# A conv-attention and expert layer for 16 images: single choice steps, half-width gate products, and w1 in reused memory

## The chip, the cores and the metric

The kernel runs on one core of one Trainium2 chip. The metric is the device time of one execution in microseconds, as the median of several runs. Everything in the kernel is float32 (or float32r, the same bits in TensorE's faster format), apart from a few bfloat16 masks.

## What is computed

The input is `x` of 16 images of 32 x 32 positions and 64 channels, so 1024 tokens of 64 channels an image. In short:

```python
# 1. convolution-style attention block
h = group_norm(x, gn_scale, gn_bias, num_groups=16)
q, k, v = nin(h, wq, bq), nin(h, wk, bk), nin(h, wv, bv)
x = x + nin(softmax(q k^T / 8) v, wo, bo)
# 2. causal attention on the layer norm
t = x.reshape(16, 1024, 64)
t = t + causal_attention(layer_norm(t), Wq, Wk, Wv)
# 3. experts choose tokens: 32 experts, 8 tokens each
u = layer_norm(t)
logits = einsum('bsd,ed->bse', u, gate_w) + gate_b
probs = softmax(logits, axis=1)            # over the 1024 tokens
topv, topi = the 8 greatest probs of each expert, and their tokens
pooled = sum over the 8 of topv * u[topi]  # (16, 32, 64)
h = gelu([pooled, 1] @ weight1[e])         # 64+1 -> 256
out = [h, 1] @ weight2[e]                  # 256+1 -> 64
t[topi] += topv * out
```

## The kernel before

The program has two parts, each a block of its own with one instruction stream an engine, ordered by semaphores; all engines meet where one block ends and the next begins. `attention_part` does steps 1 and 2, the logits, and the choice for the first three groups of images. `expert_part` does the choice of the last group, the experts, and the sum into the output.

**Turns.** `attention_part` is a pipeline over images. In turn `i` each engine walks a list written out by hand, `ORDER`, whose entries are a name and a shift: `s2.0@-1` is the piece `s2.0` for image `i - 1`. Turns run from -2 to 18. Turns 4 to 13 are a loop of five trips of two turns, in which addresses and counts are computed in registers; the others are written out. The names that matter here:

- `m1.c`, `m2.c`: TensorE products whose rows VectorE reduces to maxima (`m1r.c`, `m2r.c`, L1025), for attention 1 and 2, in the PSUM tile `maxima_in`.
- `r1`, `r2` (L589): the maxima are turned into rows in the bank `fin_ps`; `r1c`, `r2c` (L822) are ScalarE's copies to `max_rows`; `row1`, `row2` (L508) are SyncE's transfers of them into one row of `queries_lo` or `queries`. The first score of the attention, `s1.0` or `s2.0`, waits for that transfer.
- `s1.u`, `s2.u` (L677 to L681): the scores; `e1.u`, `e2.u` (L862): their exponentials on ScalarE, into `probs`; `v1.t`, `v2.t` (L696): the products with the values; `c1`, `c2` (L834) copy them.
- `ad.t` (L934): GpSimd's additions of the probabilities of attention 1; `rs1` (L597) is the product that sums them over the partitions, which waits for the last of them.
- `out1`, `out2` (L614), `f1`, `f2` (L1046), then the layer norms `l1`, `l2` on VectorE (L1054, L1059), `l1p`, `l2p` on GpSimd (L908 to L913), `l1n`, `l2n` on ScalarE (L793).
- `p2.tr` (L549), then `nh`, `nc` (L763, L766) and `nl2`, `nl1`: the normed tokens turned over into `keys`; `ya`, `yb`: the projections.
- `mtr` (L549), `ut` (L837), `mlg` (L622), `lg` (L843): the second normed tokens turned over, copied to `ut`, multiplied by the gate, and evicted with the bias to `logits`. SyncE's `sl` (L524) stores them to `logits_dram`, `su` (L518) and `st` (L513) store the normed and the plain tokens.

`ut` holds two tokens of one pair of token tiles on its 128 partitions, 64 channels each, in 512 columns. `gate_bd` is block diagonal, so that one product gives the logits of both tokens on 2 x 32 output partitions.

SyncE works its list in order too: `su@-2 st@-2 sl@-2 row2@-1 xload@+2 row1@+1`.

**The choice of experts.** Images are chosen in groups of four, so that 4 x 32 = 128 partitions hold one expert of one image each and 1024 tokens lie along a row of `lg`. The steps of a group are: `e.top` on VectorE (max of 8, its negative, match and replace, compare: L249 to L254), `e.exp` on ScalarE (L269), `e.gate` on VectorE (L257, L259), and on TensorE with a copy by ScalarE after each: `e.ta`, `e.tb` (transposes of the gates, L303), `e.pool` (64 products with `u_all`, L295), `e.turn` (L299). In turns 15 and 16 there is no image for the pieces `m1.c`, and so the choice steps of groups 0 to 2 take their places: in turn 15, two steps a piece (groups 0 and 1); in turn 16, one step a piece (group 2). A place counts from 0 to 7 in the order in which an engine's list has its `m1` pieces. Group 3 is chosen at the start of `expert_part`.

**`expert_part`.** SyncE loads the logits of group 3 (L1146), `w1` (L1148), `w2` in two halves (L1150), the bias, and the tokens `total`. TensorE waits for `w1` and for the last `e.turn`, then does the 64 hidden products (L1177), the transposes (L1188), the second products (L1198), the turn to images (L1204), and 64 products that spread the result over the tokens (L1215). VectorE adds them to `total` (L1264), and SyncE stores the output (L1163).

## Time and profile before

| | |
|---|---|
| median of 3 runs | 900.59 us (899.41 to 900.70) |
| profiled execution, its own time | 901.2 us |
| its span in the profile | 899.4 us |
| TensorE busy, share of the span | 803.9 us, 89% |
| VectorE | 566.2 us, 63% |
| ScalarE | 506.4 us, 56% |
| GpSimd | 371.0 us, 41% |
| mean TensorE clock granted | 0.941 of full speed |

The profile is of one execution. Its span runs from the first to the last instruction that the profiler shows; the time of an execution also has what lies around that. Busy time of TensorE is of pipelined instructions, whose ends are modelled. L with a number is a line of the kernel. PE is TensorE, PEld its weight loads, DVE VectorE, ACT ScalarE, POOL GpSimd, and SPq the queue of SyncE, from which the transfers are issued. What stands in brackets at the end of a row of the timeline is the time for which the engine had been idle and what released it.

### The profile page before, as it was taken

What the parts mean: (1) busy time and instruction counts of PE and PEld (TensorE: products, weight loads), DVE (VectorE), ACT (ScalarE), POOL (GpSimd) and SP (SyncE); (2) the same over time, 40 slices, a digit from 0 to 9 for tenths busy, and PEclk for the clock granted to TensorE, in tenths of its full rate; (3) what the DMA queues carried; (4) which work ended last, traced back from release to release, by engine and by line L of the source; (5) the groups of instructions that cost most, each with busy time, mean ns of one, the idle gap of its engine ahead of it and who ended that gap; (6) DMA issues with size and microseconds to landing.
All of it is one profiled execution on the core that took longest, in us unless ns stands there. A gap on an engine that the chain in (4) does not pass through costs nothing. (4 is left out here: it accounts for less than half of the span.)

```text
span 899.4 us, 14859 instructions
## 1 busy us (share of the span) xinstructions
PE 803.9 (89%) x4406; PEld 473.2 (53%) x4406; DVE 566.2 (63%) x1493; ACT 506.4 (56%) x1096; POOL 371.0 (41%) x288
## 2 busy tenths in 40 slices
PE   4586999999999999999999999999999997755286
PEld 2253556565656565656565656565656553433155
DVE  3427476767676767676767676767777755451224
ACT  3153567676767666666676666666666663533120
POOL 3062536363636364545454545455454543100000
PEclk9997899999999999999999999999999998958558
DMA  1000000000000000000000000000000020010798
GB/s 46 0 1 12 1 13 25 18 24 19 24 19 24 19 24 18 24 18 24 18 24 18 24 18 24 18 24 18 24 18 24 7 71 30 1 31 1 147 239 230
DMA packets 62997, 30.54 MB, mean 34 GB/s; under 512 B 35279, under 2 KB 60271, under 8 KB 62959
## 3 DMA queue, kind: packets, MB, share of 16 engines
q1 hardware_dynamic: 62959, 30.05, 13.5%
q8 instruction: 21, 0.34, 0.2%
q14 instruction: 17, 0.14, 0.1%
HBM read 15.23 MB, written 10.49 MB: 29 GB/s over the span
## 5 line engine op out<-in xcount | busy, mean ns | idle before, releaser
L1025 DVE TENSOR_REDUCE neg_max<-maxima_in 128x1 f32<-128x1024 f32 (+7 forms) x256 | 252.0, 984 | 94.3 <-PE maxima_in L654 90.8
L862 ACT ACTIVATE probs<-scores 128x512 f32<-128x512 f32 (+3 forms) x464 | 233.0, 541 | 118.0 <-PE scores L681 106.4
L934 POOL TENSOR_TENSOR prob_sum<-prob_sum,probs 128x1024 f32<-128x1024 f32 x96 | 228.2, 2377 | 8.8 <-ACT probs L862 0.6
L654 PE MATMUL maxima_in<-keys,queries 128*128 128x512 f32 (+3 forms) x496 | 172.6, 422 | 17.3 <-DVE neg_max L1025 14.4
L681 PE MATMUL scores<-queries,keys 128*128 128x512 f32 (+3 forms) x464 | 173.0, 373 | 0.0
L654 PEld LDWEIGHTS maxima_in<-keys,queries 128*128 128x128 f32 x496 | 85.9, 200 | 89.9 <-DVE neg_max L1025 57.4
L696 PE MATMUL values_out<-probs,x_sb 128*64 128x512 f32 x512 | 129.4, 612 | 0.0
L908 POOL TENSOR_TENSOR ln<-ln_mv,eps_ln 128x8 f32<-128x8 f32 x32 | 6.5, 203 | 297.8 <-DVE ln_mv L1059 297.8
L679 PE MATMUL scores<-queries_lo,keys_hi 65*128 65x512 f32 x256 | 109.8, 429 | 2.2 <-DMA queries_lo<-max_rows 1.2
L681 PEld LDWEIGHTS scores<-queries,keys 128*128 128x128 f32 x464 | 90.5, 195 | 8.2
L696 PE MATMUL values_out<-probs,normed 128*64 128x128 f32 (+3 forms) x480 | 84.5, 441 | 0.1
L679 PE MATMUL scores<-queries_lo,keys 128*128 128x512 f32 (+3 forms) x208 | 80.4, 388 | 0.0
L793 ACT ACTIVATE u_sb<-t,ln 128x64 f32<-128x64 f32 x128 | 44.2, 427 | 30.0 <-POOL ln L913 30.0
L679 PEld LDWEIGHTS scores<-queries_lo,keys_hi 65*128 65x128 f32 x256 | 49.8, 195 | 17.1 <-ACT probs L862 6.8
L934 POOL TENSOR_TENSOR prob_sum<-probs 128x1024 f32<-128x1024 f32 x16 | 37.8, 2361 | 50.4 <-ACT probs L862 50.4
L919 POOL TENSOR_TENSOR x_bias<-x_sb,bias_full 128x512 f32<-128x512 f32 x16 | 20.9, 1304 | 89.8 <-DVE t L1046 87.0
L696 PEld LDWEIGHTS values_out<-probs,x_sb 128*64 128x64 f32 x512 | 28.8, 136 | 53.4 <-issue 41.3
L911 POOL TENSOR_TENSOR ln<-ln,minus_half 128x8 f32<-128x8 f32 x32 | 52.6, 1642 | 0.0
L696 PEld LDWEIGHTS values_out<-probs,normed 128*64 128x64 f32 x480 | 30.2, 137 | 36.9 <-issue 26.9
L793 ACT ACTIVATE normed<-t,ln 128x63 f32<-128x63 f32 x128 | 44.0, 427 | 7.7 <-POOL ln L913 7.1
L679 PEld LDWEIGHTS scores<-queries_lo,keys 128*128 128x128 f32 x208 | 41.4, 199 | 2.4 <-ACT probs L862 0.2
L1012 DVE SCALAR_TENSOR_TENSOR keys<-proj_ps,bias_qk,keys 64x512 fp32r<-64x512 f32 x32 | 24.2, 757 | 25.5 <-ACT keys L806 25.5
(169 smaller groups left out, 1102.7 us busy)
## 6 DMA issues: line engine op xcount, KB each, us to landing
x_sb<-in_x SPq DMA_DIRECT2D x16, 256.0 KB, 2.9
u_all<-u_sb SPq DMA_DIRECT2D x16, 256.0 KB, 2.5
t_scratch<-t SPq DMA_DIRECT2D x16, 256.0 KB, 2.9
total<-t_scratch SPq DMA_DIRECT2D x16, 256.0 KB, 4.8
w_sb<-in_w SPq DMA_DIRECT2D x1, 2080.0 KB
logits_scratch<-logits SPq DMA_DIRECT2D x32, 64.0 KB, 2.1
lg<-logits_scratch SPq DMA_DIRECT2D x4, 512.0 KB, 3.7
out<-total SPq DMA_DIRECT2D x16, 128.0 KB, 2.2
```

What stands on the lines that cost most here:

```text
L654: mm = pe.matmul(maxima_in[:, lo:lo + w * P], weights, keys[s][q][:, h * HALF:h * HALF + w * P], start=not diagonal, stop=True, skip_group ...
L679: pe.matmul(shape(bank), low_keys[:, key_cols(t)], of(queries_lo[s][q]), start=not diagonal, stop=False, skip_group_check=diagonal)
L681: pe.matmul(shape(bank), keys[s][q][:, key_cols(t)], of(queries[s][q]), start=False, stop=True, skip_group_check=diagonal).then_inc(scores ...
L696: mm = pe.matmul(values_out[a * C:(a + 1) * C, j0 * P:HALF], v_sb[:, t, :], probs[:, t % NP, a * HALF + j0 * P:(a + 1) * HALF], start=t == ...
L793: ins = nc.scalar.activation(dst[:, t, 0:width], src[:, t, 0:width], ACT.Identity, bias=ln[s][:, 0, t:t + 1], scale=ln[s][:, 1, t:t + 1])
L862: nc.scalar.activation(of(probs[:, t % NP, :]), shape(scores[:, bank_of(s, u), 0:w]), ACT.Exp, scale=SCALE).then_inc(exp_done, 1)
L908: nc.gpsimd.tensor_tensor(ln[s][:, 0, :], ln_mv[s][:, :, 1], eps_ln[:, :], ALU.add).then_inc(norm_step[s], 1)
L911: nc.gpsimd.tensor_tensor(ln[s][:, 1, :], ln[s][:, 0, :], minus_half[:, :], ALU.pow).then_inc(norm_step[s], 1)
L919: nc.gpsimd.tensor_tensor(x_bias[:, :, :], x_sb[n.parity][:, :, :], bias_full[n.parity][:, :].unsqueeze(1).to_broadcast([P, NT, C]), ALU.a ...
L934: nc.gpsimd.tensor_tensor(prob_sum[:, :], before, probs[:, t % NP, :], ALU.add).then_inc(rows_added, 1)
L1012: V.scalar_tensor_tensor(out=keys[1][q][C:P, c], in0=proj_ps[C:P, :], scalar=bias_qk[C:P, 1:2], in1=keys[1][q][C:P, c], op0=ALU.add, op1=A ...
L1025: V.tensor_reduce(neg_max[s][:, at:at + 1], maxima_in[:, HALF - widths[0] * P:HALF + widths[1] * P], AX.X, ALU.max, negate=True).then_inc( ...
```

## The change

- **Choice in single steps over two turns.** `e.top` is split into `e.max`, `e.rep` and `e.ne`. A table, `EXPERT_SLOTS`, says for each engine which steps stand in which of 16 places (0 to 7 in turn 15, 8 to 15 in turn 16). Each group has its own semaphore `expert_step[k]`, and waits between groups stand where tiles are shared (`rest`, `gates_t`, the PSUM halves).
- **ScalarE's order.** `lg@-2` now stands ahead of place 0, `r2c@-1` behind place 1, and `l1n` ahead of places 5 and 6.
- **Gate product in halves.** `mlg` is two products of 256 columns, on output partitions 0 to 63 and 64 to 127; `logits` is 128 x 256, evicted in one piece; `sl` stores it in four transfers. `gate_b_sb` has 128 partitions, loaded by four transfers.
- **The last logits straight into their tile.** For image 15, `mlg` writes to partitions 96 to 127 of two banks, and `lg` puts them with two evictions into `lg`. `sl` is left out for it, and SyncE loads the other three images of group 3 right after `su` of image 15.
- **w1 into memory that is no longer read.** The tiles of attention 1 (`keys`, `queries`, `keys_hi`, `queries_lo`) lie in one region, and `w1_sb` lies over them. ScalarE issues its load after `e1.15` of image 15, in turn 15.

The diff, without what only renames semaphores:

```diff
--- before.py
+++ after.py
@@ -35,9 +36,9 @@
     "act": "e1.0 e1.1 e1.2 e1.3 e1.4 xh@+1 e1.5 e1.6 l2n@-2 e1.7 xc@+1 e1.8 e1.9 ab@+1 wh@+1 e1.10 ws@+1 e1.11 "
-        "ka.hi@+1 e1.12 e1.13 kb.hi@+1 e1.14 ut@-2 qa.hi@+1 e1.15 m1.0@+1 lg@-2 r2c@-1 m1.1@+1 c1 m1.2@+1 e2.0@-1 "
-        "e2.1@-1 m1.3@+1 e2.2@-1 qb.hi@+1 e2.3@-1 e2.4@-1 m1.4@+1 e2.5@-1 e2.6@-1 kB@+1 e2.7@-1 e2.8@-1 m1.6@+1 "
-        "l1n m1.5@+1 e2.9@-1 e2.10@-1 nh e2.11@-1 nc m1.7@+1 e2.12@-1 ya.hi c2@-1 r1c@+1 yb.hi",
+        "ka.hi@+1 e1.12 e1.13 kb.hi@+1 e1.14 ut@-2 qa.hi@+1 e1.15 lg@-2 m1.0@+1 m1.1@+1 r2c@-1 c1 m1.2@+1 e2.0@-1 "
+        "e2.1@-1 m1.3@+1 e2.2@-1 qb.hi@+1 e2.3@-1 e2.4@-1 m1.4@+1 e2.5@-1 e2.6@-1 kB@+1 e2.7@-1 e2.8@-1 l1n "
+        "m1.5@+1 m1.6@+1 e2.9@-1 e2.10@-1 nh e2.11@-1 nc m1.7@+1 e2.12@-1 ya.hi c2@-1 r1c@+1 yb.hi",
...
@@ -95,10 +96,21 @@
 NG = B // BG
-EXPERT_STEPS = ["e.top", "e.exp", "e.gate", "e.ta", "e.tb", "e.pool", "e.turn"]
-EXPERT_STEP_COUNT = {"e.top": ["max", "neg", "rest", "chosen"], "e.exp": [], "e.gate": ["recip", "gates"],
+EXPERT_STEPS = ["e.max", "e.exp", "e.rep", "e.ne", "e.gate", "e.ta", "e.tb", "e.pool", "e.turn"]
+EXPERT_STEP_COUNT = {"e.max": ["max", "neg"], "e.exp": [], "e.rep": ["rest"], "e.ne": ["chosen"], "e.gate": ["recip", "gates"],
...
+EXPERT_SLOTS = {
+    "dve": {0: [("e.max", 0)], 1: [("e.rep", 0)], 2: [("e.ne", 0)], 3: [("e.gate", 0)], 4: [("e.max", 1)], 5: [("e.rep", 1)],
+            6: [("e.ne", 1)], 7: [("e.gate", 1)], 8: [("e.max", 2)], 9: [("e.rep", 2)], 10: [("e.ne", 2)], 11: [("e.gate", 2)]},
+    "act": {2: [("e.exp", 0)], 5: [("e.ta", 0)], 6: [("e.exp", 1), ("e.tb", 0)], 7: [("e.pool", 0)], 8: [("e.turn", 0)],
+            9: [("e.ta", 1)], 10: [("e.exp", 2), ("e.tb", 1)], 11: [("e.pool", 1)], 12: [("e.turn", 1), ("e.ta", 2)],
+            13: [("e.tb", 2)], 14: [("e.pool", 2)], 15: [("e.turn", 2)]},
+    "pe": {5: [("e.ta", 0)], 6: [("e.tb", 0)], 7: [("e.pool", 0)], 8: [("e.turn", 0)], 9: [("e.ta", 1)], 10: [("e.tb", 1)],
+           11: [("e.pool", 1)], 12: [("e.turn", 1), ("e.ta", 2)], 13: [("e.tb", 2)], 14: [("e.pool", 2)], 15: [("e.turn", 2)]},
+}
...
@@ -106,11 +118,7 @@
     c = [piece for piece, _ in pieces].index(name)
-    if n == B:
-        return [(EXPERT_STEPS[k % 7], k // 7) for k in (2 * c, 2 * c + 1) if k < 14]
-    if n == B + 1 and c < 7:
-        return [(EXPERT_STEPS[c], 2)]
-    return []
+    return EXPERT_SLOTS[engine].get(c + NT * (n - B), [])
...
@@ -225,8 +233,12 @@
         pooled = sb("pooled", [C + 1, E, 32])
+        base = -(-nc.sbuf_base // 64) * 64
+        region = sb("region", [P, 8 * S + 16])
+        w1_sb = nc.alloc_sbuf_tensor_at("w1_sb", [C + 1, E, HID], F32, offset=base)
+        w1_loaded = whole.enter_context(nc.semaphore("w1_loaded"))
         logits_loaded = [whole.enter_context(nc.semaphore(f"logits_loaded{k}")) for k in range(NG)]
-        expert_step = whole.enter_context(nc.semaphore("expert_step"))
+        expert_step = [whole.enter_context(nc.semaphore(f"expert_step{k}")) for k in range(NG)]
...
@@ -236,20 +248,26 @@
-    V, step, lg, rest, top, stat, gates = (nc.vector, *(g[n] for n in ("expert_step", "lg", "rest", "top", "stat", "gates")))
+    V, lg, rest, top, stat, gates = (nc.vector, *(g[n] for n in ("lg", "rest", "top", "stat", "gates")))
+    step = g["expert_step"][k]
...
     def after(step_name):
-        before = done("expert_step", name, k, step_name, back=1)
+        before = done(f"expert_step{k}", name, k, step_name, back=1)
...
-    if name == "e.top":
-        after("max")
+    if name == "e.max":
...
         V.tensor_scalar(stat[:, k, 0:1], top[:, k, 0:1], -1.0, None, ALU.mult).then_inc(step, 1)
+    elif name == "e.rep":
+        if k > 0:
...
+            V.wait_ge(g["expert_step"][k - 1], done(f"expert_step{k - 1}", "e.gate", k - 1, "gates"))
+        after("rest")
         V.match_replace(rest[:, :], top[:, k, :], lg[:, k % 2, :], NEG_HUGE).then_inc(step, 1)
+    elif name == "e.ne":
...
@@ -283,12 +302,16 @@
-    pe, step, gates, gates_t, u_all, pool_sb, ident_f = (nc.tensor, *(
-        g[n] for n in ("expert_step", "gates", "gates_t", "u_all", "pool_sb", "ident_f")))
+    pe, gates, gates_t, u_all, pool_sb, ident_f = (nc.tensor, *(
+        g[n] for n in ("gates", "gates_t", "u_all", "pool_sb", "ident_f")))
+    step = g["expert_step"][k]
...
-    pe.wait_ge(step, done("expert_step", name, k, EXPERT_STEP_COUNT[name][0]) - 1)
+    if name == "e.ta" and k > 0:
...
+        pe.wait_ge(g["expert_step"][k - 1], done(f"expert_step{k - 1}", "e.turn", k - 1, "copy"))
+    pe.wait_ge(step, done(f"expert_step{k}", name, k, EXPERT_STEP_COUNT[name][0]) - 1)
...
@@ -325,10 +348,11 @@
-    keys = {s: [sb(f"keys{s}{q}", [P, S], F32R) for q in range(2)] for s in (1, 2)}
-    queries = {s: [sb(f"queries{s}{q}", [P, S], F32R) for q in range(2)] for s in (1, 2)}
-    keys_hi = [sb(f"keys_hi{q}", [C + 1, S], F32R) for q in range(2)]
-    queries_lo = {1: [sb(f"queries_lo1{q}", [C + 1, S], F32R) for q in range(2)],
+    in_region = lambda name, k, rows: nc.alloc_sbuf_tensor_at(name, [rows, S], F32R, offset=g["base"] + 4 * S * k)
+    keys = {1: [in_region(f"keys1{q}", q, P) for q in range(2)], 2: [sb(f"keys2{q}", [P, S], F32R) for q in range(2)]}
+    queries = {1: [in_region(f"queries1{q}", 2 + q, P) for q in range(2)], 2: [sb(f"queries2{q}", [P, S], F32R) for q in range(2)]}
+    keys_hi = [in_region(f"keys_hi{q}", 4 + q, C + 1) for q in range(2)]
+    queries_lo = {1: [in_region(f"queries_lo1{q}", 6 + q, C + 1) for q in range(2)],
...
@@ -354,7 +378,7 @@
     ut = sb("ut", [P, HALF])
-    logits = sb("logits", [2 * E, HALF])
+    logits = sb("logits", [P, HALF // 2])
...
@@ -395,7 +419,7 @@
                    (channel_consts[second, :], g["by_channel"]), (rows[:, 0, :], g["bo"]),
-                   (gate_b_sb[0:E, :], g["gate_b"]), (gate_b_sb[E:2 * E, :], g["gate_b"])]
+                   *[(gate_b_sb[r * E:(r + 1) * E, :], g["gate_b"]) for r in range(P // E)]]
...
@@ -483,15 +507,15 @@
-        def load_logits(k):
...
-            sp.wait_ge(logits_stored, 32 * (k + 1) * BG)
+        def load_logits(k, images=BG):
...
+            sp.wait_ge(logits_stored, 64 * (k * BG + images))
...
-                sp.wait_ge(g["expert_step"], done("expert_step", "e.top", k - 2, "chosen"))
+                sp.wait_ge(g["expert_step"][k - 2], done(f"expert_step{k - 2}", "e.ne", k - 2, "chosen"))
                 sp.wait_ge(g["exp_ready"], k - 1)
-            sp.dma_start(g["lg"][:, k % 2, :], logits_dram[k * BG:(k + 1) * BG].rearrange("b e s -> (b e) s")).then_inc(
-                g["logits_loaded"][k], 16)
+            sp.dma_start(g["lg"][0:images * E, k % 2, :],
+                         logits_dram[k * BG:k * BG + images].rearrange("b e s -> (b e) s")).then_inc(g["logits_loaded"][k], 16)
...
@@ -516,13 +540,15 @@
                 sp.dma_start(u_dst, u_sb[:, :, :].rearrange("p t c -> p (t c)")).then_inc(u_stored, 16)
-            elif name == "sl":
+                if n.trip is None and n.first == B - 1:
+                    load_logits(NG - 1, BG - 1)
+            elif name == "sl" and (n.trip is not None or n.first < B - 1):
...
                 sp.wait_ge(fin_step, ready)
-                dst = image_of(logits_dram, at).rearrange("e (j a t) -> a e j t", a=2, t=P)
-                for a in range(2):
-                    sp.dma_start(dst[a], logits[a * E:(a + 1) * E, :].rearrange("e (j t) -> e j t", t=P)).then_inc(
-                        logits_stored, 16)
+                dst = image_of(logits_dram, at).rearrange("e (h j a t) -> h a e j t", h=2, a=2, t=P)
+                for h, a in itertools.product(range(2), range(2)):
+                    r = (2 * h + a) * E
+                    sp.dma_start(dst[h, a], logits[r:r + E, :].rearrange("e (j t) -> e j t", t=P)).then_inc(logits_stored, 16)
...
@@ -617,9 +643,19 @@
                 transposes(fin_ps, u_sb).then_inc(fin_step, 1)
+            elif name == "mlg" and n.trip is None and n.first == B - 1:
...
+                pe.wait_ge(proj_step, done("proj_step", "yb", n, "lo"))
+                for a, bank in enumerate((fin_ps, proj_ps)):
+                    r = slice(a * C, (a + 1) * C)
+                    mm = pe.matmul(bank[P - E:P, :], gate_bd[r, a * E:(a + 1) * E], ut[r, :], start=True, stop=True)
+                mm.then_inc(fin_step, 1)
...
-                pe.matmul(fin_ps[0:2 * E, :], gate_bd[:, :], ut[:, :], start=True, stop=True).then_inc(fin_step, 1)
+                for h in range(2):
+                    mm = pe.matmul(fin_ps[h * 2 * E:(h + 1) * 2 * E, 0:HALF // 2], gate_bd[:, :],
+                                   ut[:, h * HALF // 2:(h + 1) * HALF // 2], start=True, stop=True)
+                mm.then_inc(fin_step, 1)
...
@@ -835,12 +871,20 @@
                 nc.scalar.copy(ut[:, :], fin_ps[:, :]).then_inc(fin_step, 1)
+            elif name == "lg" and n.trip is None and n.first == B - 1:
+                act.wait_ge(fin_step, done("fin_step", "mlg", n, "mm"))
+                act.wait_ge(g["expert_step"][NG - 3], done(f"expert_step{NG - 3}", "e.ne", NG - 3, "chosen"))
+                for a, bank in enumerate((fin_ps, proj_ps)):
+                    ins = nc.scalar.activation(
+                        g["lg"][P - E:P, (NG - 1) % 2, :].rearrange("p (j a t) -> p a j t", a=2, t=P)[:, a, :, :],
+                        bank[P - E:P, :].rearrange("p (j t) -> p j t", t=P), ACT.Identity, bias=gate_b_sb[P - E:P, :], scale=1.0)
+                ins.then_inc(fin_step, 1)
...
-                    act.wait_ge(logits_stored, each(n + (-1), 32))
-                nc.scalar.activation(logits[:, :], fin_ps[0:2 * E, :], ACT.Identity, bias=gate_b_sb[:, :],
+                    act.wait_ge(logits_stored, each(n + (-1), 64))
+                nc.scalar.activation(logits[:, :], fin_ps[:, 0:HALF // 2], ACT.Identity, bias=gate_b_sb[:, :],
...
@@ -861,6 +905,9 @@
                                  scale=SCALE).then_inc(exp_done, 1)
+            if s == 1 and u == len(UNITS[1]) - 1 and n.trip is None and n.first == B - 1:
...
+                nc.scalar.dma_start(g["w1_sb"][:, :, :], g["w1"].rearrange("e d h -> d e h")).then_inc(g["w1_loaded"], 16)
...
@@ -1142,10 +1189,6 @@
     def _(sp):
-        k = LAST_GROUP
-        sp.dma_start(g["lg"][:, k % 2, :], logits_dram[k * BG:(k + 1) * BG].rearrange("b e s -> (b e) s")).then_inc(
-            g["logits_loaded"][k], 16)
-        sp.dma_start(w1_sb[:, :, :], g["w1"].rearrange("e d h -> d e h")).then_inc(w1_loaded, 16)
```

## Rows read from the trace of the kernel before

**Rows 1.** Windows: busy time of each engine, weight loads second; clock; DMA.

```profile
400.00:700.00 300.00, 299.00 (x1592) 176.59 (x1593) 216.08 (x587) 202.12 (x443) 149.97 (x112) 1.00 0.08 20
...
740.00:760.00 20.00, 13.49 (x104) 6.43 (x107) 10.86 (x12) 7.13 (x13) 10.29 (x5) 0.83 0.11 33
```

**Rows 2.** The chain that ended last: start, length, what.

```profile
840.84 16.03 DMA w_sb<-in_w
...
856.91 7.05 PE hidden_ps L1177 x64
```

**Rows 3.** Timeline, start of the kernel: start, length, engine, instruction.

```profile
3.65 0.78 SPq L475 DMA_DIRECT2D gate_b_sb<-in_gate_b  x2
...
6.05 1.11 PE L549 MATMUL proj_ps<-masks_f,x_sb 128*128 128x128 f32 x4 [6.05 <-DMA gate_b_sb<-in_gate_b]
```

**Rows 4.** Timeline of TensorE in a loop turn, and one earlier row.

```profile
611.68 1.07 PE L622 MATMUL fin_ps<-ut,gate_bd 128*64 128x512 f32 x2
612.68 0.73 PE L654 MATMUL maxima_in<-keys,queries 128*128 128x512 f32 x2
...
617.55 0.23 PE L677 MATMUL scores<-mask_k,ident_b 128*128 128x128 bf16 x1
...
720.74 1.08 PE L696 MATMUL values_out<-probs,normed 128*64 128x256 f32 x8
```

**Rows 5.** Timeline of ScalarE in that loop turn.

```profile
611.91 0.59 ACT L862 ACTIVATE probs<-scores 128x512 f32<-128x512 f32 x1
612.87 0.68 ACT L843 ACTIVATE logits<-fin_ps,gate_b_sb 64x512 f32<-64x512 f32 x1 [0.37 <-PE fin_ps L622]
```

**Rows 6.** Timeline of SyncE in that loop turn.

```profile
613.72 1.48 SPq L524 DMA_DIRECT2D logits_scratch<-logits  x2
615.32 0.73 SPq L508 DMA_DIRECT2D queries<-max_rows  x1
```

**Rows 7.** Timeline: the first transfer of maxima and the score behind it.

```profile
45.14 0.78 SPq L508 DMA_DIRECT2D queries_lo<-max_rows  x1
47.08 0.28 PEld L679 LDWEIGHTS scores<-queries_lo,keys_hi 65*128 65x128 f32 x1 [1.61 <-DMA queries_lo<-max_rows]
```

**Rows 8.** Timeline of turn 3, which is written out.

```profile
205.55 1.28 SPq L524 DMA_DIRECT2D logits_scratch<-logits  x2
...
209.60 0.23 PE L677 MATMUL scores<-mask_k,ident_b 128*128 128x128 bf16 x1
```

**Rows 9.** Timelines of GpSimd, ScalarE and TensorE in turn 15.

```profile
735.97 14.89 POOL L934 TENSOR_TENSOR prob_sum<-prob_sum,probs 128x1024 f32<-128x1024 f32 x6
...
747.65 1.15 ACT L269 ACTIVATE gates<-lg,stat 128x1024 f32<-128x1024 f32 x1 [1.53 <-DVE stat L251]
...
748.80 0.67 ACT L843 ACTIVATE logits<-fin_ps,gate_b_sb 64x512 f32<-64x512 f32 x1
...
749.52 0.39 PE L589 MATMUL fin_ps<-masks_f,neg_max 128*8 128x128 f32 x2 [2.17 <-ACT logits L843]
...
760.33 0.23 PE L677 MATMUL scores<-mask_k,ident_b 128*128 128x128 bf16 x1
...
773.60 2.75 ACT L793 ACTIVATE normed<-t,ln 128x63 f32<-128x63 f32 x8
```

**Rows 10.** Timeline of SyncE at the start of the second part.

```profile
840.84 0.40 SPq L1148 DMA_DIRECT2D w_sb<-in_w  x1
841.53 16.72 SPq L1150 DMA_DIRECT2D w_sb<-in_w  x2
```

**Rows 11.** Timeline of TensorE: one group's pooling, turn 16.

```profile
814.48 1.10 PE L295 MATMUL maxima_in<-u_all,gates_t 128*32 128x64 f32 x64
```

**Rows 12.** Timeline around the change of block.

```profile
836.50 0.68 ACT L843 ACTIVATE logits<-fin_ps,gate_b_sb 64x512 f32<-64x512 f32 x1 [2.06 <-PE fin_ps L622]
...
844.18 1.23 DVE L249 MAX8 top<-lg 128x8 f32<-128x1024 f32 x1 [16.77 <-DMA lg<-logits_scratch]
...
855.80 0.26 ACT L277 COPY pooled<-small_ps 64x128 f32<-64x128 f32 x1 [0.51 <-PE small_ps L299]
```

More of the change, by code:

```diff
@@ L1 @@
+import itertools
 from contextlib import ExitStack
@@ L169, in count_increments @@
             for step in EXPERT_STEP_COUNT[name]:
-                inc("expert_step", (name, k, step))
+                inc(f"expert_step{k}", (name, k, step))
     return counts
@@ L217, in build_program @@
         ident_f = masks_f[:, 1, :]
-        gate_b_sb = sb("gate_b_sb", [2 * E, 1])
+        gate_b_sb = sb("gate_b_sb", [P, 1])
         lg = sb("lg", [P, 2, S])
@@ L263, in choose_on_scalar @@
 def choose_on_scalar(nc, g, name, k, turn, pool_ps):
-    step, gates, gates_t, pool_sb, pooled = (g[n] for n in ("expert_step", "gates", "gates_t", "pool_sb", "pooled"))
+    gates, gates_t, pool_sb, pooled = (g[n] for n in ("gates", "gates_t", "pool_sb", "pooled"))
+    step = g["expert_step"][k]
     if name == "e.exp":
-        nc.scalar.wait_ge(step, done("expert_step", "e.top", k, "neg"))
+        nc.scalar.wait_ge(step, done(f"expert_step{k}", "e.max", k, "neg"))
         nc.scalar.activation(gates[:, k, :], g["lg"][:, k % 2, :], ACT.Exp, bias=g["stat"][:, k, 0:1], scale=1.0,
@@ L271, in choose_on_scalar @@
     elif name in ("e.ta", "e.tb", "e.pool", "e.turn"):
-        nc.scalar.wait_ge(step, done("expert_step", name, k, EXPERT_STEP_COUNT[name][0]))
+        nc.scalar.wait_ge(step, done(f"expert_step{k}", name, k, EXPERT_STEP_COUNT[name][0]))
         if name == "e.pool":
@@ L536, in _ @@
         sp.wait_ge(u_stored, 16 * B)
-        sp.wait_ge(logits_stored, 32 * B)
+        sp.wait_ge(logits_stored, 64 * (B - 1))
     @block.tensor
@@ L635, in piece @@
                 name, k = in_bank.pop("step")
-                pe.wait_ge(g["expert_step"], done("expert_step", name, k, "copy"))
+                pe.wait_ge(g["expert_step"][k], done(f"expert_step{k}", name, k, "copy"))
             block_c = c if s == 1 else query_block(c)
@@ L1117, in sem @@
         return ctx.enter_context(nc.semaphore(name))
-    w1_sb = sb("w1_sb", [C + 1, E, HID])
+    w1_sb, w1_loaded = g["w1_sb"], g["w1_loaded"]
     w2_sb = sb("w2_sb", [P, E, 2, C])
@@ L1172, in _ @@
         pe.wait_ge(w1_loaded, 16)
-        pe.wait_ge(expert_step, done("expert_step", "e.turn", LAST_GROUP, "copy"))
+        pe.wait_ge(expert_step[LAST_GROUP], done(f"expert_step{LAST_GROUP}", "e.turn", LAST_GROUP, "copy"))
         for quad in range(QUADS):
```

5 lines of the change are left out of this document (3 added, 2 removed).

## The prediction

> **What bounds the kernel now.** I read the windows first. Between 400 and 700 us TensorE is busy 299.00 of 300 us at full clock [rows 1]: in the middle of the kernel, whatever takes TensorE longer, or makes it wait, is paid in full. Between 740 and 760 us it is busy only 13.49 of 20 us and its clock falls to 0.83: there the drained pipeline is bound by hand-overs. Then the chain that ended last [rows 2]: in its last 60 us it goes back to one transfer, w1, 16.03 us long, before the hidden product L1177. So four places count: the start, the loop turns, turns 15 and 16, and the tail. I read each in the timeline.
>
> **Start.** `gate_b_sb` now needs four loads instead of two. The two take SyncE 0.78 us to issue, and the first TensorE instruction waits for them at 6.05 us [rows 3]. Two more: **+0.8 us**. Nothing hides it. The bounds are 0.6 and 1.0.
>
> **The logits in each turn: product, eviction, stores.** Before, the product L622 holds TensorE from 611.68 to 612.68 us, two passes of 512 columns on 64 output columns [rows 4]. Now it is two products of 256 columns, each on its own half of the output partitions. The nearest row is eight such passes in 1.08 us [rows 4], so four take about 0.5: TensorE gains 0.5 us a turn, if nothing else holds it. It gains nothing if the halves run one after the other.
>
> The eviction L843 starts at 612.87 and takes 0.68 us [rows 5]. With an earlier product it can start when the exponential before it ends, 611.91 + 0.59 = 612.50, and 256 fewer elements a partition save some 0.2 us: it ends near 613.01, not 613.55, 0.54 us sooner. Bounds: 0.2 and 0.6.
>
> The stores grow from two to four on SyncE, and `row2`, the transfer of the maxima of attention 2, stands behind them in SyncE's order. In a loop turn two issues take 1.48 us [rows 6]; two more add 1.49. `row2` was issued at 615.32 and now goes at 615.32 - 0.54 + 1.49 = 616.27. What such a transfer takes is seen once, where TensorE waits for it: issued at 45.14, work begins at 47.08 [rows 7], 1.94 us, and I take 1.9. So before, `row2` landed near 617.22 and `s2.0` began at 617.55 [rows 4] without a wait, 0.33 us to spare. Now it lands near 618.17, while TensorE, 0.5 us earlier, would be there at 617.05. The wait swallows the half microsecond and makes the turn 0.62 us longer. Behind `s2.0` in TensorE's order stand all scores, values and out1, and behind those VectorE's f1 and l1, so it isn't made up. The loop has 10 turns: **+6.2 us**. The other three turns (2, 3, 14) are written out and have no register work between the issues: two take 1.28 us, and `s2.0` follows at 209.60 [rows 8]. Four end near 205.55 - 0.54 + 2.62 = 207.63, the row lands near 209.5, in time: 0. Bounds of the whole term: with issues of 0.39 us as in [rows 3] the row is hidden and 13 turns give up to -5; with no gain from the product and eviction it is +12. I stay with 0.74 an issue, since it is the same tile and destination.
>
> The Trainium skill (DMA: Bandwidth & Descriptors, section on the anatomy of one DMA, written for GpSimd's path) puts the sequencer's dispatch at about 50 ns and calls descriptor generation small; by that, two more stores would cost SyncE 0.1 us and the row would stay hidden, which is the second case below. The rows of this case show 0.6 to 0.7 us an issue, ten times that.
>
> **Turn 15 (no image 16; experts of groups 0 and 1).** Before, ScalarE does the first choice's exponential at 747.65, waiting for VectorE's max, before the eviction of the logits at 748.80; the product `r2` at 749.52 waits for that eviction, and `s2.0` of image 14 begins at 760.33, behind a gate product, transposes and the pooling [rows 9]. Now the eviction stands ahead of the choice, and TensorE's first expert step comes at slot 5, after `v2.1`. What is late next is GpSimd: its last row addition ends at 735.97 + 14.89 = 750.86 [rows 9], the row sums wait for it, and `row2` behind four stores lands near 751.6. So `s2.0` begins near 752.0: -8.3. Between there and the layer norm L793 at 773.60 [rows 9] the second group's max, replace, compare and exponential leave the path too: VectorE's single steps fall in the gaps between f1, l1 and nl2, ScalarE's copies come behind that norm. I get it near 762; but then copy, exponential of group 1 and a second copy (0.6 + 1.3 + 0.6) stand ahead of the next projections' eviction, so that from there on the lead is **-10.2 us**. If w1's traffic delays `row2` by 3 us it is -7; if nothing of the copies counts, -12.
>
> **w1.** Its load is now issued by ScalarE after `e1.15` of image 15. On SyncE the issue took 0.40 us [rows 10]; behind it ScalarE's queue has the logits' eviction, for which `r2` waits, with 4 us to spare against GpSimd's end. I cost it at nothing. The memory it lands in was the first attention's keys and queries, dead by then.
>
> **Turn 16.** Moved here: pooling and turning of group 1, with group 2's steps later. Of it, TensorE's pooling is 1.10 us [rows 11] (up to 1.9 at the lower clock), the turn 0.3, and group 2's transposes now wait for ScalarE's copy of that turn, some 0.5 beyond what the score banks cost anyhow: about 2 us. Two extra copies on ScalarE before `row2`'s source cost 0.3. **+2.3 us**, bounds 0.5 and 4.5. VectorE's steps there lie in its idle time beside the scores.
>
> **Tail.** Before: the logits' eviction ends at 836.50 + 0.68 = 837.18, and the max of group 3 starts at 844.18, after store, block change and load [rows 12]: 7.0 us. Now three images are loaded during the layer norm's tail, and image 15 goes from the two banks into the tile. That adds a second product (its rows and bank differ; 0 to 2 us, I take 0.5), a second eviction 0.6 and a block change 0.3: 1.4 us, so -5.6. From max to the last copy, 855.80 + 0.26 = 856.06 [rows 12], nothing changes; then w1 was waited for until 856.91 [rows 2], which goes: -0.85. **-6.4 us**, bounds -4 and -7. What is late next is w2, but it is needed only behind the 7.05 us of L1177 and the transposes, and now isn't queued behind w1. The sums and output stores keep their pace.
>
> **Sum.** 0.8 + 6.2 - 10.2 + 2.3 - 6.4 = -7.3 us. The profiled execution took 901.2 us (span 899.4 and 1.8 around it), 0.6 above the median of 900.59. 901.2 - 7.3 = 893.9, as a median **893.3 us**.
>
> **The rivals.**
>
> 1. The row is late in the loop: 893.3, own range 888 to 898. For it: 1.49 us of issue against 0.33 of slack. Chance 0.50.
> 2. The row stays hidden, since an issue with half the blocks is shorter or the transfer lands sooner. Then the loop gives -5 instead of +6.2: 893.3 - 11.2 = 882. With partial hiding 887. For it: [rows 3] has issues of 0.39. Chance 0.27.
> 3. w1's transfer, 16 us on the same DMA engines, holds up `row2` of image 14 (and the late row costs more than I think): +3, some 896 to 898. The Trainium skill (DMA: Bandwidth & Descriptors, "Issuing engines are not separate DMA queues") says that transfers issued by different engines interleave on the same 16 engines. No row of before has such a small transfer beside a large one of another queue. Chance 0.10.
> 4. The final choice doesn't start sooner, because the block's end still waits for stores: only w1's 0.85 of the tail is gained, 899. Against it: only the stores of the tokens remain, which are issued ahead of the logits. Chance 0.06.
> 5. Slower: ScalarE is held while it issues w1. The two w2 loads held SyncE for 16.72 us [rows 10]. In turn 15 ScalarE has some 4 us of cover; each further one goes onto the end, so above 4 + 7.3, about 11 us, the kernel is slower; at 16.7 it is 906. Against it: w1's own 0.40. Chance 0.07.
>
> **Chances and range.** Faster by over 0.2%: cases 1 to 4, less a little for mishaps, 0.91. Within 0.2%, which is about what a measurement of this kernel can tell from no change: 0.02. Slower: 0.07. The range reaches down to case 2 and up to cases 3 and 4: 882 to 900.
>
> **What would show it.** The first TensorE instruction at 6.8 us. In loop turns four issues of L524's successor over 2.9 us, and `s2.0` waiting some 1.1 us for the DMA of `max_rows`; each such turn 0.62 us longer. The logits' product at 0.5 us. In turn 15, `s2.0` of image 14 near 1.2 us behind GpSimd's last addition, and not ten. The max of group 3 1.4 us after the last eviction, L1177 with no DMA wait. The prediction is wrong if the wait at `s2.0` isn't there (then near 882), if ScalarE's w1 issue is longer than a few us, or if the block change waits.

## The result, and the profile after

The changed kernel takes **884.28 us** as the median of 4 runs (882.52 to 888.38), the kernel before 900.64 beside it (899.41 to 902.65). The ratio is 0.9824, with a 95% interval of 0.9800 to 0.9849. The forecast was 893.3 us, with a range of 882 to 900. The sign was right and the time lies in the range, but the gain is 16.4 us, more than twice the 7.3 that the sum gave. A second set of runs of the same kernel gave 888.46 (884.72 to 891.23) against 900.26, ratio 0.9864 (0.9825 to 0.9902). Over the eight runs of both sets the mean is 886.5.

The profiled execution took 884.59 us, with a span of 882.8. In the middle of the kernel the windows view looks as in [rows 1] (busy time of TensorE, its weight loads, VectorE, ScalarE and GpSimd, then clock, DMA share and GB/s): TensorE is the bound, at full clock. From 740 to 760 us the clock and TensorE's busy time are a little lower than in [rows 1], and the DMA share has gone from 0.11 to 0.65. That is w1's transfer, which now lies in this stretch.

```profile
400.00:700.00 300.00, 299.01 (x1614) 177.63 (x1616) 217.89 (x589) 202.72 (x446) 152.40 (x113) 1.00 0.08 20
...
740.00:760.00 20.00, 12.75 (x63) 7.12 (x62) 9.78 (x21) 6.77 (x14) 7.70 (x4) 0.74 0.65 140
```

**A loop turn.** First TensorE's timeline, then SyncE's, of the changed kernel, in the turn of [rows 4] and [rows 6].

```profile
609.97 0.65 PE L656 MATMUL fin_ps<-ut,gate_bd 128*64 128x256 f32 x4
610.56 0.73 PE L690 MATMUL maxima_in<-keys,queries 128*128 128x512 f32 x2
...
615.42 0.23 PE L713 MATMUL scores<-mask_k,ident_b 128*128 128x128 bf16 x1
```

```profile
611.39 1.84 SPq L551 DMA_DIRECT2D logits_scratch<-logits  x4
613.34 0.69 SPq L532 DMA_DIRECT2D queries<-max_rows  x1
```

The product takes 0.59 us of TensorE from its start to the next, not 1.00 as in [rows 4]. Four stores take 1.84 us, 0.46 each, where two took 1.48. (A block is 128 tokens of one expert that lie together; a store had 32 x 4 = 128 of them and has 64 now.) `row2` is issued 1.95 us after the first store instead of 1.60, and `s2.0` at 615.42 has no idle time in brackets: it didn't wait. Counted from the start of the gate product, the first store is 0.62 us sooner than before (1.42 instead of 2.04), so `row2` is 0.27 us sooner (3.37 instead of 3.64) and `s2.0` 0.42 (5.45 instead of 5.87).

**Turn 15.** TensorE's timeline, ScalarE's queue, SyncE's, and what the DMA view of 742 to 762 us says.

```profile
748.28 1.08 PE L623 MATMUL fin_ps<-prob_sum,ones_f 128*32 128x256 f32 x8 [2.77 <-POOL prob_sum L981]
753.83 0.29 PE L713 MATMUL scores<-mask_k,ident_b 128*128 128x128 bf16 x1 [4.47 <-DMA queries<-max_rows]
```

```profile
742.78 0.63 ACTq L910 DMA_DIRECT2D w_sb<-in_w  x1
```

```profile
745.90 0.65 SPq L532 DMA_DIRECT2D queries<-max_rows  x1
```

```profile
q10 hardware_dynamic: 2093, 2.13, 52.1%
q1 hardware_dynamic: 480, 0.66, 12.9%
```

Here is a wait that the forecast sum doesn't have. `s2.0` of image 14 stands 4.47 us for a row of 4 KB, issued at 745.90 and usable at 753.83: 7.9 us instead of the 1.9 of [rows 7]. In the second trace it stands 5.29 us. In that stretch w1's queue, q10, takes 52% of the DMA engines' time.

**The change of part and the tail.** VectorE's and ScalarE's timelines, then the chain that ended last.

```profile
831.03 0.66 ACT L878 ACTIVATE lg<-proj_ps,gate_b_sb 32x512 f32<-32x512 f32 x1
```

```profile
832.04 1.23 DVE L261 MAX8 top<-lg 128x8 f32<-128x1024 f32 x1 [10.66 <-PEq L243]
```

```profile
844.21 4.84 PE hidden_ps L1220 x64
...
852.91 4.15 PE small_ps L1241 x128
...
860.08 15.82 PE hidden_ps L1258 x64
```

The max of group 3 follows the end of the last eviction by 0.35 us; it was 7.0 in [rows 12]. Nothing of w1 stands in the chain any more, and the hidden product takes 4.84 us, not the 7.05 of [rows 2]; this difference is also seen without an edit (after_again, below).

**The span cut up.** The gate's product (`mlg`) of image 0, 13, 14 and 15 and the hidden product cut each trace into six stretches. Each row is one profiled execution, in us; the numbers are differences of start times in TensorE's timeline. The kernels are those of the experiments below.

| kernel | to image 0 | 0 to 13 | 13 to 14 | 14 to 15 | 15 to hidden product | to the end | span |
|---|---|---|---|---|---|---|---|
| before | 158.49 | 586.93 | 52.84 | 36.23 | 22.42 | 42.5 | 899.4 |
| after | 160.68 | 581.99 | 48.15 | 37.66 | 15.73 | 38.6 | 882.8 |
| after, again | 158.64 | 581.77 | 48.34 | 37.26 | 16.03 | 43.9 | 885.9 |
| halves_only | 160.62 | 581.68 | 51.57 | 35.62 | 21.82 | 44.2 | 895.5 |
| no_halves | 158.57 | 586.96 | 49.15 | 38.25 | 15.99 | 44.4 | 893.3 |
| no_w1 | 159.50 | 581.87 | 43.18 | 36.66 | 18.86 | 43.8 | 883.9 |
| w1_later | 159.98 | 581.61 | 41.99 | 37.37 | 15.88 | 44.1 | 880.9 |
| no_steps | 160.73 | 581.98 | 51.45 | 35.46 | 15.96 | 40.7 | 886.3 |
| no_last | 160.67 | 582.03 | 48.55 | 37.44 | 20.85 | 42.2 | 891.7 |
| eight_stores | 158.57 | 615.53 | 48.13 | 38.19 | 15.97 | 41.2 | 917.6 |
| eight_row_first | 160.40 | 581.46 | 46.04 | 37.29 | 15.88 | 44.0 | 885.1 |
| best1 | 159.80 | 581.65 | 41.58 | 37.68 | 15.86 | 38.7 | 875.3 |
| best1, again | 158.13 | 581.85 | 40.65 | 37.63 | 16.21 | 44.2 | 878.7 |
| best2 | 158.99 | 581.59 | 42.01 | 37.31 | 16.05 | 43.9 | 879.9 |

The first and the last stretch differ by up to 2.6 and 5.8 us whatever the edit, and between executions of one kernel as well. The four in between repeat within 0.4 us in the two executions of the changed kernel and within 0.9 in those of best1, and in them the parts of the change can be read one by one.

### The profile page after: what moved, and what is told of

Same layout as the page of the kernel before. It is cut to its first block and busy times, and to the rows that moved or that the text cites. A ratio compares the mean times of both kernels' runs of the same rounds, so it can differ in the third digit from the quotient of the medians.

```text
span 882.8 us, 14997 instructions
## 1 busy us (share of the span) xinstructions
PE 796.8 (90%) x4438; PEld 474.7 (54%) x4438; DVE 564.6 (64%) x1493; ACT 503.7 (57%) x1097; POOL 370.2 (42%) x288
## 5 line engine op out<-in xcount | busy, mean ns | idle before, releaser
L717 PE MATMUL scores<-queries,keys 128*128 128x512 f32 (+3 forms) x464 | 175.1, 377 | 0.0
L732 PE MATMUL values_out<-probs,x_sb 128*64 128x512 f32 x512 | 127.5, 608 | 0.0
L829 ACT ACTIVATE u_sb<-t,ln 128x64 f32<-128x64 f32 x128 | 44.2, 428 | 29.9 <-POOL ln L960 29.9
L732 PEld LDWEIGHTS values_out<-probs,x_sb 128*64 128x64 f32 x512 | 28.5, 135 | 53.3 <-issue 38.7
L829 ACT ACTIVATE normed<-t,ln 128x63 f32<-128x63 f32 x128 | 44.1, 426 | 9.0 <-POOL ln L960 9.0
```

The lines of the kernel that those rows point to most:

```text
L717: pe.matmul(shape(bank), keys[s][q][:, key_cols(t)], of(queries[s][q]), start=False, stop=True, skip_group_check=diagonal).then_inc(scores ...
L732: mm = pe.matmul(values_out[a * C:(a + 1) * C, j0 * P:HALF], v_sb[:, t, :], probs[:, t % NP, a * HALF + j0 * P:(a + 1) * HALF], start=t == ...
L829: ins = nc.scalar.activation(dst[:, t, 0:width], src[:, t, 0:width], ACT.Identity, bias=ln[s][:, 0, t:t + 1], scale=ln[s][:, 1, t:t + 1])
```

## The experiments

**halves_only**: only the product, eviction and four stores of the change; choice steps, last logits and w1 as before.

```diff
-            if s == 1 and u == len(UNITS[1]) - 1 and n.trip is None and n.first == B - 1:
-                nc.scalar.dma_start(g["w1_sb"][:, :, :], g["w1"].rearrange("e d h -> d e h")).then_inc(g["w1_loaded"], 16)
+        sp.dma_start(w1_sb[:, :, :], g["w1"].rearrange("e d h -> d e h")).then_inc(w1_loaded, 16)
...
+EXPERT_SLOTS = {engine: OLD_SLOTS for engine in ("dve", "act", "pe")}
...
-            elif name == "mlg" and n.trip is None and n.first == B - 1:
...
-            elif name == "lg" and n.trip is None and n.first == B - 1:
```

The first pair is no_w1 below, the second no_steps, the third no_last.

> The changed kernel with three of its parts undone: choice steps as before, last logits by way of memory, w1 loaded in the second part. Left of the change: gate product in halves, four stores of logits, four loads of the bias, and attention 1's tiles in one region. Theory A (a store with half the blocks is issued in some 0.46 us, so the row of maxima stays hidden and TensorE keeps its half microsecond a turn): 900.6 + 0.5 at the start - 13 x 0.43 = 895.5, with s2.0 of the loop turns without a wait. Theory B (the prediction's: the row is late in the loop): 907. Theory C (the loop's gain comes from something else than the halves, the tiles' place in memory): 895.5 too, and the next kernel tells it from A.

Measured: 897.1 us (ratio 0.9959, 0.9943 to 0.9975). The stretch from image 0 to 13 is 581.68 us, 5.25 shorter than before, with no wait for the row in a loop turn. The halves give 0.4 us a turn; the late row of the forecast isn't there. (907 would have been the time with it.)

**no_halves**: the change without them.

```diff
-                for h in range(2):
-                    mm = pe.matmul(fin_ps[h * 2 * E:(h + 1) * 2 * E, 0:HALF // 2], gate_bd[:, :],
-                                   ut[:, h * HALF // 2:(h + 1) * HALF // 2], start=True, stop=True)
+                pe.matmul(fin_ps[0:2 * E, :], gate_bd[:, :], ut[:, :], start=True, stop=True).then_inc(fin_step, 1)
```

> The changed kernel with the gate product whole again and two stores of logits of 64 x 512; all else stays. Theory A: the loop turns are 45.35 us again, not 44.93; 884.3 + 5 = 889. Theory C (tiles' place in memory): the turns stay at 44.93 and the time at 884 to 885.

Measured: 894.8 us (0.9923, 0.9897 to 0.9949). 586.96 us from image 0 to 13, the number of before to 0.03. (The 889 us of the forecast are 6 short.) So the loop's gain comes from the halves alone, and not from the tiles' new place in memory or anything else that moved. The whole time is 8.3 us above the changed kernel's mean of 886.5. The two profiled executions differ by more, 10.5 us, twice what the loop accounts for; the table puts 5.8 of it into the last stretch, where the clock differed (below).

**no_w1**: w1 loaded at the start of the second part again. **w1_later**: ScalarE issues it after the first exponential of attention 2 of image 14, which is behind the row that it held up.

```diff
-            if s == 1 and u == len(UNITS[1]) - 1 and n.trip is None and n.first == B - 1:
+            if s == 2 and u == 0 and n.trip is None and n.first == B - 2:
                 nc.scalar.dma_start(g["w1_sb"][:, :, :], g["w1"].rearrange("e d h -> d e h")).then_inc(g["w1_loaded"], 16)
```

> The changed kernel with w1 loaded by SyncE at the start of the second part, ahead of w2, into the same memory. Theory D (w1's traffic holds up the row of maxima of image 14 in turn 15, which landed 7.9 us after its issue): that transfer lands in 2 us, s2.0 of image 14 waits no more than 0.3 us for it, which gives back 4.4 us; and the hidden product waits for w1 until some 16.5 us after the second part's start, 4 us longer than now, and runs at the lower clock again, 2.2 us more. Sum 884.3 - 4.4 + 4 + 2.2 = 886. Rival E (the row was late for another reason, four stores ahead of it): s2.0 still waits 4 us, 890.

> The changed kernel with ScalarE's issue of w1 moved behind the first exponential of attention 2 of image 14, so behind the row of maxima of that turn. Theory D: s2.0 of image 14 starts at once behind the row sums, 4.4 us earlier, and nothing small is in flight while w1 lands: 884.3 - 4.4 = 880. Rival E: no change, 884. A third way: the transfer now collides with the loads of logits of group 2, which isn't needed for 40 us, so no cost.

Measured: 884.98 us (0.9824, 0.9803 to 0.9845) and 879.34 us (0.9762, 0.9745 to 0.9779). TensorE's timeline of w1_later in turn 15:

```profile
747.21 1.08 PE L623 MATMUL fin_ps<-prob_sum,ones_f 128*32 128x256 f32 x8 [2.78 <-POOL prob_sum L981]
748.22 0.29 PE L713 MATMUL scores<-mask_k,ident_b 128*128 128x128 bf16 x1
```

`s2.0` follows the row sums without a gap. From image 13 to 14 it is 43.18 us without w1 and 41.99 with w1 later, against 48.15 and 48.34 in the two traces of the changed kernel: w1's transfer costs 5.0 to 6.4 us there. In no_w1 some 3 us come back in the tail (18.86 us from the last gate product to the hidden one, against 15.73 and 16.03), where the chain that ended last holds the transfer again:

```profile
824.87 15.15 DMA w_sb<-in_w
840.07 7.05 PE hidden_ps L1218 x64
```

So w1 at the chosen place gains nothing that the times show over not moving it; issued seven microseconds later, at 749.60, it gives a median 5 us lower.

**no_steps**: the old cutting of the choice into seven steps a turn apart, and ScalarE's old order. The table of slots becomes:

```diff
+OLD_STEPS = [["e.max", "e.rep", "e.ne"], ["e.exp"], ["e.gate"], ["e.ta"], ["e.tb"], ["e.pool"], ["e.turn"]]
+OLD_SLOTS = {c: [(name, k // 7) for k in (2 * c, 2 * c + 1) if k < 14 for name in OLD_STEPS[k % 7]] for c in range(8)}
+OLD_SLOTS.update({8 + c: [(name, 2) for name in OLD_STEPS[c]] for c in range(7)})
```

> The changed kernel with the old cutting of the choice (seven steps a turn apart, the gate's value and the exponentials after it on the old turns) and ScalarE's old order. Theory E (the choice as single operations takes GpSimd's product out of the way of the last images' softmax sums): the stretch between the gate products of images 13 and 14, 52.8 us before and 48.2 after, goes back to about 52.5, and w1's transfer hides in it; the loop keeps its period of 44.9. 884.3 + 4.5 = 889. Rival: the row behind w1's transfer sets that stretch whichever way the choice is cut: 884 to 885.

Measured: 887.83 us (0.9857, 0.9819 to 0.9896). 13 to 14 takes 51.45 us, 3.3 more than with the new steps, and 14 to 15 takes 35.46, 2.2 less. In the interval of the times it can't be told from the changed kernel. The theory had 52.5 us for the first of these stretches and 889 for the whole. With w1 in the way, the new steps are worth about 1 us. Without it they are worth much more: halves_only has the old steps and 51.57 + 35.62 = 87.2 us, no_w1 the new ones and 79.8. With the old steps w1's early load costs nothing (51.45 us with it, 51.57 in halves_only without): `s2.0` comes so late there that the row is in place.

**no_last**: the last image's logits stored and loaded back like the others.

```diff
-            elif name == "mlg" and n.trip is None and n.first == B - 1:
...
-            elif name == "lg" and n.trip is None and n.first == B - 1:
...
-                if n.trip is None and n.first == B - 1:
-                    load_logits(NG - 1, BG - 1)
...
+        sp.dma_start(g["lg"][:, k % 2, :], logits_dram[k * BG:(k + 1) * BG].rearrange("b e s -> (b e) s")).then_inc(
+            g["logits_loaded"][k], 16)
```

> The changed kernel with the last image's logits stored and loaded back as the others, the load at the head of the second part. Theory F (the gap at the change of parts is the round trip of the last logits): the last choice starts 7.0 us after the last eviction and not 0.35, so +6.65 and some 0.7 for the plain store: 891. Rival (the load of w1 and w2 would be awaited at the second part's start anyway): 884 to 886; against it stands that w1 is already there and w2 is wanted only 8 us later.

Measured: 891.17 us (0.9883, 0.9845 to 0.9920). VectorE's timeline:

```profile
837.26 1.23 DVE L261 MAX8 top<-lg 128x8 f32<-128x1024 f32 x1 [15.66 <-DMA lg<-logits_scratch]
```

The eviction ended at 829.86 + 0.47 = 830.33, so the gap is 6.9 us again; from the last product to the hidden one it is 20.85 us instead of 15.73 to 16.03. Doing without the round trip through memory is worth 5 us.

**eight_stores** and **eight_row_first**: each turn's logits in eight stores of 32 blocks, with SyncE's order as it is and with `row2` ahead of the stores.

```diff
-                for h, a in itertools.product(range(2), range(2)):
+                for h, a, j in itertools.product(range(2), range(2), range(2)):
                     r = (2 * h + a) * E
-                    sp.dma_start(dst[h, a], logits[r:r + E, :].rearrange("e (j t) -> e j t", t=P)).then_inc(logits_stored, 16)
+                    sp.dma_start(dst[h, a, :, j, :], logits[r:r + E, j * P:(j + 1) * P]).then_inc(logits_stored, 16)
```

```diff
-    "sp": "su@-2 st@-2 sl@-2 row2@-1 xload@+2 row1@+1",
+    "sp": "su@-2 st@-2 row2@-1 sl@-2 xload@+2 row1@+1",
```

> The changed kernel with each turn's logits stored in eight transfers of 32 blocks instead of four of 64. Two and four stores took 0.74 and 0.46 us of SyncE each. Theory G (an issue has a fixed part of about 0.18 us and 0.0044 us a block, from 128 blocks in 0.74 and 64 in 0.46): 8 x 0.32 = 2.6 us, row2 issued 0.7 us later than now, at the edge of hidden, so the loop moves by 0 to +0.3 us a turn: 884 to 889. Rival (an issue costs the same 0.46 us whatever it holds): 3.7 us a turn, row2 1.8 us later, TensorE waits 1.0 to 1.8 us at s2.0 in each turn: 884 + 13 x 1.4 = 902.

> Eight stores of 32 blocks again (922 us with the stores ahead of row2), and SyncE's order swapped so that row2's issue goes ahead of the stores. Theory G2 (all of the 37 us that eight stores added is the row that arrives 2 us late in each turn; the stores themselves hold up nobody): the turn goes back to 44.9 us and the time to 884 to 887. Rival (the small transfers themselves, 64 blocks more per turn on the queue and on SyncE, slow the loop): over 900.

Measured: 922.03 us (1.0240, 1.0205 to 1.0274) and 885.78 us (0.9819, 0.9789 to 0.9850). The theory's slope over blocks was wrong, and the rival's price was nearly right (0.50 us a store for 0.46); but the rival's time, 902, was 20 us short. SyncE's and TensorE's timelines of eight_stores:

```profile
636.38 3.99 SPq L551 DMA_DIRECT2D logits_scratch<-logits  x8
640.48 0.68 SPq L532 DMA_DIRECT2D queries<-max_rows  x1
```

```profile
642.54 0.22 PE L713 MATMUL scores<-mask_k,ident_b 128*128 128x128 bf16 x1 [1.97 <-DMA queries<-max_rows]
```

Here is the late row that the forecast expected, with its mark in brackets, 2.06 us behind its issue. It makes the 13 turns 615.53 - 581.99 = 33.5 us longer, 2.6 us a turn, more than the 1.8 that TensorE waits per turn at this place from 400 to 700 us. The windows from image 0 to 13, of the changed kernel and of eight_stores, and three microseconds behind one of the waits, say where the rest is:

```profile
160.68:742.67 581.99, 579.68 (x3115) 341.11 (x3114) 419.49 (x1144) 388.00 (x850) 293.38 (x220) 1.00 0.09 22
158.57:774.10 615.53, 591.78 (x3115) 351.03 (x3114) 420.06 (x1144) 388.76 (x850) 293.33 (x220) 0.98 0.09 21
...
690.00:693.00 3.00, 3.00 (x13) 2.81 (x13) 1.27 (x7) 1.11 (x2) 0.00 (x0) 0.50 0.18 41
```

TensorE has the same 3115 products on record, but is idle 23.8 us instead of 2.3 and busy 591.8 instead of 579.7. So 21.4 of the 33.5 us are the waits, and 12.1 are the same work at a lower clock: behind seven of the loop's ten waits the granted clock falls to 0.50 for some microseconds. With the row ahead of the same eight stores the 13 turns are back at 581.46, so the small transfers themselves cost nobody anything. Between 13 and 14 eight_row_first still stands behind w1:

```profile
752.52 0.29 PE L713 MATMUL scores<-mask_k,ident_b 128*128 128x128 bf16 x1 [3.97 <-DMA queries<-max_rows]
```

**best1**: w1_later, with the four `gate_b` loads behind the second image and a semaphore of their own, for which only `lg` waits. **best2**: best1 with `row2` ahead of the stores.

```diff
-                   *[(gate_b_sb[r * E:(r + 1) * E, :], g["gate_b"]) for r in range(P // E)]]
+                   ]
...
         sp.dma_start(x_sb[1][:, :, :], xv[1]).then_inc(x_loaded[1], 16)
+        for r in range(P // E):
+            sp.dma_start(gate_b_sb[r * E:(r + 1) * E, :], g["gate_b"]).then_inc(gate_b_loaded, 16)
...
             elif name == "lg":
+                act.wait_ge(gate_b_loaded, 64)
```

> w1 issued by ScalarE after the first softmax piece of image 14 (as in w1_later, 879.3) and the four loads of gate_b behind the second image, on a semaphore of their own that only the first eviction of logits waits for. The four loads took 1.71 us of SyncE ahead of TensorE's start at 6.59. Theory H (the first wait ends with the last of these loads, and the whole kernel follows it): TensorE starts at 4.9 to 5.2 and all else 1.4 us sooner: 878. Rival (the start is bound by the 256 KB image that lands at about 5.9 whatever stands behind it): 879.

> best1 (w1 behind the first softmax piece of image 14, gate_b off the start) with row2's issue ahead of the four stores. max_rows is ready at 612.99 in the turn where the row is now issued at 613.34, and the first scores start at 615.42, 0.03 us after the row lands. Theory (the row is just hidden with four stores): nothing to gain in the loop, at most 0.1 us a turn, 877 to 879. Rival (the row is what the turn waits for, and TensorE's order merely hides it): 0.3 us a turn sooner, 873 to 875.

Measured: 878.73 us (0.9761, 0.9722 to 0.9800) and 881.48 (0.9776, 0.9750 to 0.9802). TensorE starts at 5.82 us in best1 (6.26 when it ran again) instead of 6.59, its wait now ended by the load of `bo`; SyncE's 1.7 us don't come back in full, and in the time nothing shows: w1_later has the same ratio. The intervals of w1_later and best1 lie below those of the changed kernel, or just touch them: over its two sets best1 has a mean of 878.3 us in eight runs, where the changed kernel has 886.5. best2 gains nothing over it: its median is some 3 us higher (best1 had 877.82 in the same set), which neither of its forecasts had and which stays unexplained. Its 581.59 us from image 0 to 13 say that with four stores the row is hidden.

**best1_again** and **after_again**: the same two kernels once more.

> The kernel of best1 once more (878.7 us). Theory K (the granted clock of the second part differs from one execution to the next of the same kernel, hidden product 4.95 or 7.05 us, the 128 small products behind it 4.14 or 6.97): the profiled execution may stand at either level and the runs spread over 4 to 6 us. Rival (the clock there is set by the kernel's edits): hidden product 4.95 and small products 4.14 again.

> The changed kernel once more (884.3 us; hidden product 4.84 us, small products 4.15 in its profile). Theory K: either level in the profiled execution. Rival: 4.84 and 4.15 again.

Measured: 877.82 us (0.9737, 0.9711 to 0.9762) and 888.46 (0.9864, 0.9825 to 0.9902). Both profiled executions show the longer tail this time. The windows of the changed kernel's hidden product, 128 small products and sums, in its first trace:

```profile
844.21:849.05 4.84, 4.84 (x65) 2.87 (x66) 0.00 (x0) 2.95 (x4) 0.00 (x0) 0.74 1.00 275
852.91:857.06 4.15, 4.12 (x129) 4.01 (x128) 0.69 (x1) 0.00 (x0) 0.00 (x0) 0.91 1.18 292
860.08:875.90 15.82, 15.80 (x64) 13.64 (x64) 10.38 (x15) 0.00 (x0) 0.00 (x0) 0.89 0.55 157
```

and in its second:

```profile
842.04:849.09 7.05, 7.05 (x65) 3.40 (x65) 0.00 (x0) 2.95 (x4) 0.00 (x0) 0.50 1.14 291
852.96:859.93 6.97, 6.95 (x129) 6.84 (x128) 0.69 (x1) 0.00 (x0) 0.00 (x0) 0.50 0.50 123
862.96:879.25 16.29, 16.27 (x64) 13.95 (x64) 10.38 (x15) 0.00 (x0) 0.00 (x0) 0.86 0.55 157
```

It is the same kernel and the same work: the three pieces take 24.8 us in one execution and 30.3 in the other, 5.5 us apart. Time multiplied by the granted clock is nearly the same in both (3.6, 3.8 and 14.1 against 3.5, 3.5 and 14.0), so the clock accounts for it: half speed (1.2 GHz) through the first two in one execution, rising to full (2.4 GHz) in the other. best1 likewise had a hidden product of 4.95 us in its first trace and 7.05 in its second. So no edit is needed for the difference.

## Why the prediction was right and wrong

| term | forecast | profiled execution | where it was isolated |
|---|---|---|---|
| start | +0.8 | +0.5 to first TensorE instruction | best1: no effect on the time |
| loop and written-out turns | +6.2 | -4.9 | halves_only -5.25, no_halves +0.03 against before |
| turn 15 | -10.2 | -4.7 | -9.7 without w1, -10.9 with w1 later |
| turn 16 | +2.3 | +1.4 | no_steps: 2.2 |
| tail, to the hidden product | -6.4 | -6.7 | no_last: 5.1 of it |
| last stretch | 0 | -3.9 | after_again: none of it (+1.4) |
| drift ahead of image 0 | 0 | +2.2, the start in it | after_again: +0.15 |

The column of the profiled execution adds up to -4.9 - 4.7 + 1.4 - 6.7 - 3.9 + 2.2 = -16.6, the difference of the spans (the start is in the drift). Without the two stretches that change from one execution to the next it is -14.9. The mean of the changed kernel's eight runs lies some 14 us below that of the kernel before in the same two sets. Against the forecast of -7.3 the loop is off by 11.1 us one way and turn 15 by 5.5 the other. That the time still fell into the range is thus in part luck.

**The loop: wrong, and this decided it.** The step that failed is the price of a store: "I stay with 0.74 an issue, since it is the same tile and destination." The same tile was now cut into stores of half the blocks, and those took 0.46 each. Four cost 1.84 us, not 2.97, so the row went out 0.35 us later relative to the first store, where 1.49 was forecast, and the earlier product and eviction (0.62 us) more than pay for that. The wait at `s2.0` that the +6.2 stands for isn't there, and the loop gained 4.9 us. The mechanism behind the step stands: with eight stores the row is 2 us late, TensorE waits at `s2.0`, and the loop loses even more than it waits, since the clock falls behind the wait. The product's gain, taken as 0.5 us, was 0.41. Rival 2 described this case, its -5 for the loop is what came, and it had 0.27 where the late row had 0.50. A hint was there: [rows 3] has short issues of 0.39, and I set them aside; so the rows didn't show "0.6 to 0.7 us an issue" throughout. Had the term been taken as -5, the sum would have been -18.5, and its 882 would have been 2 us off for the wrong reason, as the next point shows.

**Turn 15: mechanism right, w1's cost at nothing wrong.** With w1 out of the way the stretch is 9.7 to 10.9 us shorter than before, where the text had -10.2; some 1.3 of that comes without the new order (halves_only). From the gate product of image 13 to `s2.0` w1_later takes 748.22 - 741.59 = 6.63 us, before it was 760.33 - 745.42 = 14.91: -8.3, the text's own number. The forecast looked for w1's cost in its issue on ScalarE (0.63 us in the profile, harmless): "I cost it at nothing." The transfer it left to a bound and to rival 3, at +3 and a chance of 0.10. It came in both traces and costs 5.0 to 6.4 us. The Trainium skill (DMA: Bandwidth & Descriptors, "Issuing engines are not separate DMA queues") says that transfers of all issuing engines interleave on the same 16 DMA engines. The trace agrees: the 4 KB row took 7.9 us beside w1. With the row issued even ahead of the stores (eight_row_first) the wait is still 3.97 us, so it is w1 and not the place in SyncE's queue.

**Turn 16: right.** 2.2 us in no_steps, 1.4 against before, for 2.3.

**Tail: right to 0.3 us.** From the end of the first eviction to the max it is 832.04 - 831.12 = 0.92 us where 1.4 was expected, with the second eviction in it: the two products on their own banks ran at the same time (both start at 828.48), and no time for the block change was seen. The w1 wait went. From the max to the end of the last copy it is 12.0 us, against 11.9 before.

**Last stretch: not in the forecast.** In the profiled execution TensorE's clock was higher in the tail, -3.9 us; in the second trace it was not, and the stretch was 1.4 us longer than before.

**Rivals 4 and 5** didn't come: the final choice starts sooner, and ScalarE's queue is held 0.63 us, not 16.7.

What stays open: why a store gets cheaper from 128 to 64 blocks and not from 64 to 32, what makes the stretch ahead of image 0 differ by 2 us, and what leads an execution into one or the other clock level in the tail.

## What to carry to other kernels

Where a count of transfers doubles and each gets half the blocks, bound the issue time by the shortest row of the same engine as well as by the same tile's. If the slack behind it (here 0.3 us) is used up by one price and not by the other, give both cases equal weight. A large transfer put early onto an idle queue isn't free: look for the next small transfer that something waits for, and issue the large one behind it; here seven microseconds were worth 5 us. When a busy engine is made to wait once a turn, look at the granted clock behind the wait as well as at the wait. Before a tail of a few microseconds is put down to an edit, profile the same kernel twice.
